# State-space chunks on TensorE: the state in four quarters over 128 partitions, B and C as one operand, row squares summed by TensorE, D on ScalarE, two buffers for the gate

## The reference, cut to what matters

```
z, xBC, dt = split(u @ in_w.T)             # 1024, 1024 + 32 + 32, 32 columns
xBC = silu(causal conv of 4 taps over the tokens (xBC) + conv_b)
xh, Bm, Cm = split(xBC)                    # 32 heads x 32, 32, 32
state = exp(dt * A) * state + (dt * x) B   # per head, token by token
y = state @ C + D * xh
y = y * silu(z)
y = y * rsqrt(mean(y * y) + eps) * rms_w
out = y @ out_w.T
```

## Time and profile before

| | |
|---|---|
| median of 3 runs | 1617.61 us (1614.58 to 1622.73) |
| the profiled execution | 1618.92 us, span 1617.4 us |
| PE, weight loads | 80%, 56% of the span |
| DVE, ACT, POOL | 67%, 46%, 21% |
| mean granted clock of PE | 0.893 |
| chunk loop, first layer | from about 170 us to 420 us of the span |
| chunk loop, second layer | from about 476 us to 728 us |

### The profile page before, as it was taken

The page is one execution under the profiler, slowest core; times in us unless marked ns, Lnnn a source line. Parts: engine busy times, 40 slices in busy tenths (PEclk is TensorE's granted clock), DMA queues, the critical chain, the costliest instruction groups (busy, mean ns, idle before and its releaser), DMA issues.

```text
span 1617.4 us, 34487 instructions
## 1 busy us (share of the span) xinstructions
PE 1297.6 (80%) x12750; PEld 899.7 (56%) x12751; DVE 1079.4 (67%) x1659; ACT 747.7 (46%) x1123; POOL 341.7 (21%) x365
## 2 busy tenths in 40 slices
PE   3735699988368999965569999756999999999991
PEld 2215576765266766723245555354677777776770
DVE  3676778887658888867876676563646774477333
ACT  2238466464556466422452323242556664466330
POOL 0112334534313534520220000014000000000004
PEclk9757799999689999987779999955999999999996
DMA  8133000000310000014120000036425663354005
GB/s 289 39 145 108 9 3 2 1 1 2 137 34 4 2 1 2 1 52 157 63 79 1 0 0 0 0 121 260 169 104 214 233 228 128 130 197 162 26 26 162
DMA packets 35639, 133.10 MB, mean 82 GB/s; under 512 B 8120, under 2 KB 9912, under 8 KB 25600
## 3 DMA queue, kind: packets, MB, share of 16 engines
q1 hardware_dynamic: 27424, 104.04, 17.7%
q0 software_dynamic: 8160, 28.32, 5.2%
HBM read 109.67 MB, written 22.68 MB: 82 GB/s over the span
## 4 chain that ended last, share of the span: by engine, by line
PE 48%; DVE 22%; issue 12%; ACT 6%; POOL 6%; DMA 5%; DVEq 0%; POOLq 0%; SPq 0%; ACTq 0%
PE banks L2133 14%; PE banks L2154 14%; DVE mb_ca L607 6%; PE banks L1665 4%; PE banks L1695 3%; PE banks L975 2%; PE banks L999 2%; POOL mb_ysq L903 1%; POOL xs_table L2166 1%; POOL mb_ring L926 1%; POOL mb_quad L931 1%; DMA eb_un<-ys_table,eb_slot 1%; DVE mb_S L676 1%; PE banks L340 1%; PE banks L1068 1%
## 5 line engine op out<-in xcount | busy, mean ns | idle before, releaser
L2133 PE MATMUL banks<-eb_x_hi,eb_w_hi 128*128 128x128 f16 x1344 | 228.9, 220 | 2.1 <-DVE eb_x_lo L2033 2.1
L2133 PE MATMUL banks<-eb_x_lo,eb_w_hi 128*128 128x128 f16 x1344 | 228.8, 220 | 0.0
L2133 PE MATMUL banks<-eb_x_hi,eb_w_lo 128*128 128x128 f16 x1344 | 228.8, 220 | 0.0
L975 PE MATMUL banks<-mb_u_hi,mb_wi_hi 128*128 (+3 forms) x1152 | 203.8, 222 | 29.7 <-ACT mb_sz L830 15.5
L975 PE MATMUL banks<-mb_u_hi,mb_wi_lo 128*128 (+3 forms) x1152 | 203.2, 221 | 0.0
L975 PE MATMUL banks<-mb_u_lo,mb_wi_hi 128*128 (+3 forms) x1152 | 203.1, 221 | 0.0
L607 DVE SCALAR_TENSOR_TENSOR mb_ca<-mb_xp,mb_par,mb_ca 128x128 f32<-128x128 f32 x384 | 159.1, 477 | 6.0 <-ACT mb_ca L799 4.0
L975 PEld LDWEIGHTS banks<-mb_u_hi,mb_wi_hi 128*128 128x128 f16 (+1 forms) x1152 | 113.9, 99 | 47.6 <-issue 46.2
L2133 PEld LDWEIGHTS banks<-eb_x_hi,eb_w_hi 128*128 128x128 f16 x1344 | 132.5, 99 | 4.8 <-issue 2.5
L2133 PEld LDWEIGHTS banks<-eb_x_lo,eb_w_hi 128*128 128x128 f16 x1344 | 132.5, 99 | 2.4
L2133 PEld LDWEIGHTS banks<-eb_x_hi,eb_w_lo 128*128 128x128 f16 x1344 | 132.5, 99 | 0.0
(11 more groups left out here) (433 smaller groups left out, 3113.6 us busy)
## 6 DMA issues: line engine op xcount, KB each, us to landing
eb_raw<-e_w SPq DMA_DIRECT2D x36, 1024.0 KB, 5.4
eb_un<-e_w SPq DMA_DIRECT2D x28, 1024.0 KB, 7.7
mb_ring<-m_in_w SPq DMA_DIRECT2D x8, 1072.0 KB, 6.0
xs_table<-zero POOLq DMA_DIRECT2D x1, 6400.0 KB, 20.7
eb_xg<-xs_table POOLq DMA_DIRECT2D x23, 256.0 KB, 2.9
ys_table<-eb_y POOLq DMA_DIRECT2D x21, 256.0 KB, 6.5
ab_raw<-a_in_w SPq DMA_DIRECT2D x4, 1154.0 KB, 12.3
mb_ring<-m_out_w SPq DMA_DIRECT2D x4, 1024.0 KB, 5.2
```

What stands on the lines that cost most here:

```text
L975: x = e.matmul(ps[0:width, bank, n * P:(n + 1) * P], a[:, k, f:f + width], b[:, k, ds(i * P, P)], start=(k == 0 and m == 0), stop=(k == KD ...
L2133: o = e.matmul(ps[:, j, c * P:(c + 1) * P], a[:, side, k, f * P:(f + 1) * P], b[:, k, :], start=(k == 0 and m == 0), stop=(k == KD - 1 and ...
```

## The change

The state S and its faded copy are held as 128 partitions by 256 columns: quarter q of the heads on partitions 32q to 32q + 31. B and C are one operand of 64 partitions, projected, convolved and put through Silu as one. SP copies the 32 rows of C by four DMAs a chunk into `cdiag`, 128 partitions by 4x128 columns, zero outside its four diagonal blocks; PE's scores and its state product read C from there, so that a chunk's PE body now waits for those DMAs. The state product is 2 matmuls over 128 partitions with 512 columns instead of 8 over 32 with 128, and B times x is 4 matmuls of 256 columns to four quarters instead of 2 of 512. The state update stands ahead of the last conv taps on DVE, and the row statistics behind it. The squares are summed by 8 accumulating matmuls in place of three POOL additions and one matmul. D times x is 8 scaled copies on ACT. The gate has two buffers, used in turn (`side`), so that its Silu no longer waits for the gate product; the loop on each engine therefore runs over pairs of chunks. On POOL the conv of B and C goes ahead of the power. The weight ring is free from the first chunk of a layer on. The diff, cut:

```diff
-    edec, dte = sb("edec", [P, TT, H2]), sb("dte", [P, TT, H2])
+    edec, dte = sb("edec", [P, TT, H2 // 4]), sb("dte", [P, TT, H2])
...
-    xc, bcc = sb("xc", [P, JD, P]), sb("bcc", [NS, 2, P])
-    sz = sb("sz", [P, JD, P])
+    xc, bcc = sb("xc", [P, JD, P]), sb("bcc", [2 * NS, P])
+    part = sb("part", [2 * NS, TAPS - 1, P])
+    cdiag = sb("cdiag", [P, 4, P])
+    sz = sb("sz", [P, 2, JD, P])
...
-    S = sb("S", [NS, DI])
+    S, faded = sb("S", [P, DI // 4]), sb("faded", [P, DI // 4])
...
+            def c_rows(g):
+                e.wait_ge(bcc_done, g + 1)
+                core.apart(e)
+                for q in range(4):
+                    e.dma_start(cdiag[q * NS:(q + 1) * NS, q, :], bcc[NS:2 * NS, :]).then_inc(c_in, 16)
...
             with e.Fori(1, TT) as i:
                 e.wait_ge(diff, l * (TT * MB_EG) + i * MB_EG)
                 core.apart(e)
                 pair_rows(i)
+                c_rows(l * TT + i)
...
-                    e.tensor_tensor(yi.rearrange("p j t -> p (j t)"), ps[:, 5:7, :].rearrange("p b n -> p (b n)"),
-                                    ec.rearrange("p j t -> p (j t)"), ALU.mult).then_inc(yi_done, 1)
+                    e.tensor_tensor(by_half(yi), ps[:, 5:7, :].rearrange("p h (q t) -> p h q t", q=4), by_half(ec), ALU.mult)\
+                        .then_inc(yi_done, 1)
...
-                    e.tensor_tensor(S[:], faded, ps[0:NS, 3:5, :].rearrange("p b n -> p (b n)"), ALU.add).then_inc(s_done, 1)
+                    e.tensor_tensor(S[:], faded[:], ps[:, 3, 0:DI // 4], ALU.add).then_inc(s_done, 1)
 
                 def last_rows():
                     if not is_first:
                         add_rows(i - 1, g - 1)
                     from_state()
+                    next_state()
+                    if not is_first:
+                        row_stats(i - 1, g - 1)
...
-                next_state()
...
-                e.tensor_tensor(y, y, sz[:], ALU.mult).then_inc(y_done, 1)
-                if not is_first:
-                    row_stats(i - 1, g - 1)
+                e.tensor_tensor(y, y, sz[:, side, :, :], ALU.mult).then_inc(y_done, 1)
...
-                own(e.activation(edec[:], ps[:, 3, TT * H2:2 * TT * H2].rearrange("p (i h) -> p i h", i=TT), ACT.Exp))
+                for q in range(4):
+                    rows = slice(q * NS, (q + 1) * NS)
+                    x = e.activation(edec[rows, :, :], ps[rows, 3, TT * H2:2 * TT * H2].rearrange("p (i h) -> p i h", i=TT)
+                                     [:, :, q * 8:q * 8 + 8], ACT.Exp)
+                own(x)
...
+            def skip(g):
+                e.wait_ge(xc_done, 2 * (g + 1))
+                for j in range(JD):
+                    x = e.activation(dx[:, j, :], xc[:, j, :], ACT.Copy, scale=par[:, MB_DCOL + j:MB_DCOL + j + 1])
+                x.then_inc(dx_done, 1)
...
                 else:
                     grow(g - 1)
+                    skip(g - 1)
                     e.wait_ge(xtr, g)
                     e.wait_ge(dx_done, g)
...
-            def project_z(g, is_first):
-                if not is_first:
-                    e.wait_ge(y_done, g)
+            def project_z(g, side):
...
-            def sum_squares(g):
-
-                e.wait_ge(ysq_done, g + 1)
-                for k, half in enumerate((4, 2, 1)):
-                    e.tensor_tensor(ysq[:, 0:half, :], ysq[:, 0:half, :], ysq[:, half:2 * half, :], ALU.add)\
-                        .then_inc(ysum_done, 1)
-                    e.wait_ge(ysum_done, 3 * g + (k + 1))
...
-                if not is_first:
-                    sum_squares(g - 1)
-                e.wait_ge(xc_done, 2 * (g + 1))
-                e.tensor_tensor(dx, xc[:], par[:, MB_DCOL:MB_DCOL + JD].unsqueeze(2).to_broadcast([P, JD, P]), ALU.mult)\
-                    .then_inc(dx_done, 1)
+                if not is_last:
+                    conv_bc(g + 1)
                 if not is_first:
                     power(g - 1)
-                if not is_last:
-                    conv_bc(g + 1)
                 e.wait_ge(dx_done, g + 1)
                 e.wait_ge(yi_done, g + 1)
                 e.tensor_tensor(yi, yi, dx, ALU.add).then_inc(yid_done, 1)
...
-                project(i, 0, [MB_CB, MB_CC], NS, bc_mm)
+                project(i, 0, [MB_CB], 2 * NS, bc_mm)
...
-                e.wait_ge(ysum_done, 3 * g + 3)
-                e.matmul(ps[:, 2, 384:385], ysq[:, 0, :], core.ones[:, 0:1], start=True, stop=True).then_inc(rms_mm, 1)
+                e.wait_ge(ysq_done, g + 1)
+                for j in range(JD):
+                    x = e.matmul(ps[:, 2, 384:385], ysq[:, j, :], core.ones[:, 0:1], start=(j == 0), stop=(j == JD - 1))
+                x.then_inc(rms_mm, 1)
...
-                e.wait_ge(bcc_done, g + 1)
+                e.wait_ge(c_in, (g + 1) * 64)
                 if not is_first:
                     e.wait_ge(ya_done, g)
                 core.apart(e)
-                e.transpose(ps[:, 2, 0:NS], bcc[:, 0, :], core.ident[0:NS, 0:NS])
-                e.matmul(ps[:, 2, P:2 * P], bcc[:, 0, :], bcc[:, 1, :], start=True, stop=True).then_inc(g_mm, 1)
+                e.transpose(ps[:, 2, 0:NS], bcc[0:NS, :], core.ident[0:NS, 0:NS])
+                e.matmul(ps[:, 2, P:2 * P], bcc[0:NS, :], cdiag[0:NS, 0, :], start=True, stop=True).then_inc(g_mm, 1)
...
-                for j in range(JD):
-                    x = e.matmul(ps[:, 5 + j // 4, (j % 4) * P:(j % 4 + 1) * P], S[:, j * P:(j + 1) * P], bcc[:, 1, :],
+                for half in range(2):
+                    x = e.matmul(ps[:, 5 + half, :], S[:, half * P:(half + 1) * P], cdiag[:].rearrange("p q t -> p (q t)"),
                                  start=True, stop=True)
                 x.then_inc(inter_mm, 1)
                 e.wait_ge(ec_done, g + 1)
-                for q in range(2):
-                    x = e.matmul(ps[0:NS, 3 + q, :], btok[:], xe[:, q * 512:(q + 1) * 512], start=True, stop=True)
+                for q in range(4):
+                    x = e.matmul(ps[q * NS:(q + 1) * NS, 3, 0:DI // 4], btok[:], xe[:, q * (DI // 4):(q + 1) * (DI // 4)],
+                                 start=True, stop=True)
```

More of the change, by code:

```diff
@@ L458, in chunks, with few_heads, by_half @@
     def chunks(e, l, body):
-        body(0, l * TT, True, False)
-        with e.Fori(1, TT - 1) as i:
-            body(i, l * TT + i, False, False)
-        body(TT - 1, l * TT + TT - 1, False, True)
+        body(0, l * TT, True, False, 0)
+        with e.Fori(0, TT // 2 - 1) as r:
+            body(r * 2 + 1, l * TT + r * 2 + 1, False, False, 1)
+            body(r * 2 + 2, l * TT + r * 2 + 2, False, False, 0)
+        body(TT - 1, l * TT + TT - 1, False, True, 1)
+    def few_heads(x):
+        return x.rearrange("p (h q) -> p h q", h=H2 // 4)
+    def by_half(x):
+        return x.rearrange("p (q h) t -> p h q t", h=2)
     def heads(x):
@@ L870, in pool @@
         e.wait_ge(pool_own, 1)
+        e.memset(cdiag[:], 0.0)
         with e.Fori(0, LAYERS) as l:
@@ L874, in pool @@
             e.memset(S[:], 0.0)
[L875 removed]
+            e.memset(bcp[:, 0:3], 0.0)
             e.memset(xp[:, :, 0:3], 0.0).then_inc(zeroed, 1)
@@ L885, in conv_bc @@
                 core.apart(e)
-                w = par[0:NS, MB_BCW:MB_BCB].rearrange("p (c k) -> p c k", c=2)
-                part = [ysq[0:NS, 2 * k + 2:2 * k + 4, :] for k in range(TAPS - 1)]
                 for k in range(TAPS - 1):
-                    x = e.tensor_tensor(part[k], bcp[:, :, k:k + P], w[:, :, k].unsqueeze(2).to_broadcast([NS, 2, P]), ALU.mult)
+                    x = e.tensor_tensor(part[:, k, :], bcp[:, k:k + P],
+                                        par[0:2 * NS, MB_BCW + k:MB_BCW + k + 1].to_broadcast([2 * NS, P]), ALU.mult)
                 x.then_inc(pool_own, 1)
@@ L939, in body @@
                 e.tensor_tensor(yi, yi, dx, ALU.add).then_inc(yid_done, 1)
-                if is_last:
-                    e.wait_ge(s_done, g + 1)
-                    core.apart(e)
-                    e.sem_inc(ring_free, 1)
-                else:
+                if not is_last:
                     keep_halo(g + 1)
             chunks(e, l, body)
-            sum_squares(l * TT + TT - 1)
             power(l * TT + TT - 1)
```

66 lines of the change are left out of this document (34 added, 32 removed).

## The result

The changed kernel takes **1652.67 us** (median of 4 runs, 1649.97 to 1653.45), the kernel before beside it 1616.32 us (4 runs, 1614.58 to 1622.73): 1.0215 times as long, 95% interval 1.0183 to 1.0246. The forecast was 1624 us, range 1604 to 1642. It is slower, and slower than the range (whether by 2% or more, the interval leaves open).

A forecast was written before the change was run, and what follows sets the result against it. Two engines, PE and DVE, were taken as nearly full, with a loop of hand-overs setting the 30.2 us period. Steady transitions −1.2, first chunks +1 and last chunks +6.5 sum to +6.3, giving 1624 us, range 1604 to 1642.

The forecast's parts named there:

- four DMAs 2.8 us: Ahead of PE's scores: the four copies of C take 2.8 us, ends 2.2 and 3.5.
- three further issues of 0.35: Within the DMA wait: each DMA after the first adds 0.35 us of issue time on SP.
- rival 3: PE's idle time becomes one 2 us stretch per chunk and its clock falls: 1660 us; chance 0.05.
- 1.75 for D on ACT: Last chunk of each layer: ACT's eight copies for D make POOL's sum end 1.75 us later.
- Conv's end: DVE's last conv steps in a steady chunk end at 290.5 instead of 289.98, +0.55 us.
- Rival 1: PE ahead of the scores: DMA time beyond 2.9 us goes whole into each transition; 1631 to 1638 us; chance 0.27.
- 1.5 for the row sum: Each layer's end: the last row sum's 14 extra PE passes are bare, +1.5 us.
- 0.5 for a first chunk: First chunk of each layer: three more Exp of a quarter's decay, less a shorter first, +0.5 us.
- the 2.7 that I had thought PE would get back: First chunks: scores start 2.7 us later for the DMAs, regained through cheaper B × x and no gate wait: 0.
- the row sum's 16 passes: PE's sum of squares: 16 f32 passes instead of 2, 1.5 us more (up to 2.9), loads taking 1.7 us.
- B × x overlapping: PE's four B × x outputs in different array quarters take between 0.5 us, if overlapping, and 1.7; hidden either way.
- 0.39: The stated chance that the changed kernel is slower, beside faster 0.18 and same 0.43.

The follow-up runs named there:

- e1_first_block: The changed kernel with the scores waiting only for the first of the four DMAs, the other three awaited ahead of the state product: 1610.52 us.
- e8_gate_dmas: The kernel before with two gate buffers plus the four DMAs of C into an unread buffer, which PE awaits ahead of the scores: 1646.72 us.
- e6_pool_skip: The changed kernel with ACT writing C's four blocks instead of the DMAs, and D times x back on POOL: 1597.59 us.
- e3_fill: The changed kernel with 13 unused f16 matmuls of 512 columns behind the gate's projection, keeping PE at work during the DMA wait: 1641.19 us.
- e4_gate_alone: The kernel before with two gate buffers and nothing else of the change: 1603.49 us.
- e9_early: The changed kernel, DMAs included, with only ACT's Silu of B and C issued ahead of the two of x: 1580.24 us.

## Why the prediction was wrong, point by point

I put the steady transition into steps; from the rows at full clock, beside what the prediction had (changes against before, in us):

| | predicted | measured | how |
|---|---|---|---|
| first M product to row sum | +1.2 | +1.3 | 14.90 (306.88 − 30.67 to 291.11) for 13.58 |
| row sum to conv's end | −0.3 | −0.8 | 8.30 for 9.10 |
| conv's end to B, C ready | −0.1 | −0.1 | 0.86 for 0.97 |
| B, C ready to scores | +1.5 | **+2.5** | 3.91 for 1.44 |
| scores to copy of B | −2.4 | −2.4 | 0.56 for 2.96 |
| copy of B to first M product | 0 | 0 | 2.14 for 2.15 |
| sum | −0.1 | +0.5 | 30.67 for 30.20 |

- **The failed step is "four DMAs 2.8 us".** With 0.1 to start the scores that was 2.9; it measured 3.91, beyond its upper end (3.5, with the 0.1 3.6) as well. The landing was near (1.8 for 1.67). What failed is "three further issues of 0.35": an issue takes 0.59, so four take 2.48. I took the price from a single DMA to DRAM and gave it no range of its own. This adds 1.0 a chunk, 12 us over the twelve transitions. It alone gives 1636, still inside the range. The Trainium skill (DMA: Bandwidth & Descriptors, Issuing engines are not separate DMA queues) says that the sequencer's time to initiate a DMA is usually small relative to the DMA; here one issue takes 0.59 us for a landing of 1.8, and four (2.48) take longer than the landing of the last, and the measurement decides. The Trainium skill's about 2.0 us fixed, which the prediction cites (DMA: Bandwidth & Descriptors, Anatomy of one DMA, for the GpSimd path), is near the 1.8 that the landing took here, on SP.
- **The second is rival 3, "the clock falls", at 0.05 and left out of the range. It is what took the time beyond the range.** It argued from the sum of PE's idle time: 1.00 is held with 2.4 us of it per period. That time was scattered, 1.40 the longest. Now 3.17 us lie in one piece ahead of the scores, of 4.0 in all. In the steady chunks the clock was held with 2.1 us of idle time per period, 1.24 of them ahead of the scores (e1_first_block), and fell in some with 3.4 and 2.58 (e8_gate_dmas) and with 4.0 and 3.17. The two grow together, so which of them matters isn't shown, nor why the later transitions of a layer are spared. Seven of the fourteen distances of the changed kernel were hit, 16.6 us in all. The price was right: 3 us for a piece of 7 us, where the pieces of 6.8 us cost 3.0 to 3.3. The prediction named the stretch, and named its length 2 us, so the DMA term entered here once more.
- **The last chunks were costed without the DMAs.** The last distance of a layer grew by 4.0 us (24.3 to 28.3, 24.4 to 28.4), for which I had 1.75 for D on ACT. The wait ahead of the scores lies in this distance too, and the sum had it in the twelve steady transitions and not in the last two. (D's own 1.75 was too much: taking D off ACT shortened a last distance by 1.1, e6_pool_skip.) With the early Silu, and D still on ACT, the last distances are 23.8 and 24.2.
- **Conv's end was too late.** After the row sum I had 8.8 us, it took 8.3: ACT's eight copies for D took 2.44 us, not 2.85, so POOL's sum and conv behind it came earlier.
- **Rival 1 had the mechanism and the place right, but not its threshold** ("Every us beyond 2.9 for the four transfers goes whole into each transition"). With 2.00 us instead of 3.91 between B and C ready and the scores the period fell by 1.94 (e1_first_block), as whole below 2.9 as above it. That the period is off by 0.6 us and not by 1.0 is luck: conv's end, 0.5 earlier than I had it, hides half of the miss.
- **The whole sum, by the two traces.** They are 34.5 us apart where I had 6.3. The 28.2 between are, but for rounding: 16.6 for the falls of the clock (the loops of the changed kernel against those of e3_fill), 5.9 for the twelve transitions (+12 by the DMAs, −6 by conv's earlier end), 3.9 for the last distances, 5.4 for the stretch between the layers, 1.1 ahead of the first gate product, and −4.8 behind the loops.
- **The stretch between the layers** grew by 7.4 us, where I had 1.5 for the row sum and 0.5 for a first chunk. By DVE's timelines: +1.4 up to the row sum, as predicted; +2.7 from there to a reciprocal, ahead of which DVE stands still for 3.27 us instead of 0.54; +2.1 from there to the evaluation of the decay sums, before which ACT waits 3.1 us for PE instead of 1.1 and has 0.5 more of Exp; +3.6 up to the first scores, which wait for the first chunk's DMAs; and −2.2 from there on, of the 2.7 that I had thought PE would get back. The +2.7 has nothing to do with the DMAs or the state: the kernel before with two gate buffers, whose loop runs over pairs too, has it as well, and so have all the versions. What DVE waits for there the profile doesn't show. The rows of the kernel before, the changed one and e4_gate_alone:

```profile
422.88 0.20 DVE L570 RECIPROCAL mb_rstd<-mb_rstd 128x8 f32<-128x8 f32 x1 [0.54 <-ACT mb_rstd L757]
```

```profile
440.72 0.20 DVE L586 RECIPROCAL mb_rstd<-mb_rstd 128x8 f32<-128x8 f32 x1 [3.27 <-issue]
```

```profile
415.14 0.20 DVE L571 RECIPROCAL mb_rstd<-mb_rstd 128x8 f32<-128x8 f32 x1 [3.18 <-issue]
```

- **Sized right**: the row sum's 16 passes (1.84 us for 1.7), B × x overlapping (0.64, between the 0.5 and 1.7 given), the state product, the update of 0.41 ahead of the taps, the gate's Silu ahead of the product, PE's wait for a DMA.
- **The chances**: the parts give 0.40 for slower (0.27, 0.05 and 0.08), not 0.39; this changes nothing.
- **Not seen**: that the two parts fight. PE has 0.6 us less to do by the gate's buffers, 2.1 less by the operand and the quarters, and 1.55 more by the squares; I costed each by the path of the next chunk, where a DMA wait hid both. Once that is gone, PE's work plus 0.9 to 1.6 us of waits is the period in the nine versions that don't wait for DMAs in a steady chunk.

**What stays open**: DVE's 3.1 to 3.4 us ahead of the reciprocal in every version with loops over pairs, and the 2.1 us ahead of the decay sums. PE's time at the lower clock between the layers went from 44 to 58 us by the trace's record, but it is 58 in versions with 104 us and 44 in others with 99 to 100 us for that stretch, so it goes along with the time, and which causes which wasn't tried. Nor was it tried which of the two, the operand or the quarters, gives how much of PE's 2.1 us.

## What to carry to other kernels

Before pricing a new transfer on a path, look when its source is ready, and when the engine that issues its producer is idle: here the input lay ready while ACT waited for something else, and four lines moved up were worth 72 us. The Trainium skill has this as a rule (DMA: Bandwidth & Descriptors, Rules for kernel authors: issue the DMA early, wait on its semaphore late), and e9_early agrees with it, with its 3.2 us of wait going to none in a steady chunk. When a kernel is near one engine's work, write down that engine's work and its idle time per period for each edit apart: equal periods may hide a gain and a loss, and the worth of an edit measured alone (2.0 us for the gate buffer) may be 0.2 beside the others. And an idle stretch that a change puts into TensorE's work is to be priced twice, as time and as a risk for the clock: here the second took 16.6 us.

## What the runs showed of the hardware that I had not expected

- Small SBUF-to-SBUF DMAs (16 KB) take SP 0.59 us each to issue (565 to 624 ns over the 64 of the changed kernel), where the 192 KB one to DRAM took 0.36; the landing is 1.8 us.
- ACT reads partitions 32 to 63 and writes any of the four quarters: four copies of 32x128 through Silu take 1.27 us, a third of the 3.9 that the DMAs took for the same.
- Matmuls that write to four different quarters overlap: eight passes of B × x took 0.64 us, where three passes of twice the columns took 1.47.
- DVE's twelve conv steps take 3.91 us where the end of them lies beside POOL's conv of B and C (from 288.16) and 3.49 in the kernel before, without it; the gate product takes 2.02 beside POOL's fading of the state and 1.22 without.
- The clock can fall and return in the midst of a loop whose chunks are all alike: each fall lasted 3.4 or 6.8 us, and the distances with one were 1.6 to 3.3 us longer.
